# Deformable convolution: a strip sampled in six units instead of two halves, with three weight buffers and the positions on VectorE

## The reference, cut to what matters

```
y0, x0 = floor(yp), floor(xp)            # yp, xp: pixel + tap (ky, kx) + learned offset, 8 groups x 9 taps
val = gather(y0, x0) * (1 - wy) * (1 - wx) + gather(y0, x0 + 1) * (1 - wy) * wx
    + gather(y0 + 1, x0) * wy * (1 - wx) + gather(y0 + 1, x0 + 1) * wy * wx
val = val * mask                         # one mask per pixel, group and tap
out = einsum('bhwkc,kcf->bhwf', val, weight) + bias
out = relu(out) + fine_cal; result = x + out
```

## Time and profile before

| | us |
|---|---|
| median of 3 runs | 3745.19 |
| lowest and highest run | 3737.2 and 3747.83 |
| the profiled execution's own time | 3750.21 |
| its span, first to last instruction | 3748.5 |
| mean granted TensorE clock in it | 0.956 |

### The profile page before, as it was taken

The page is one execution under the profiler, slowest core; times in us unless marked ns, Lnnn a source line. Parts: engine busy times, 40 slices in busy tenths (PEclk is TensorE's granted clock), DMA queues, the critical chain, the costliest instruction groups (busy, mean ns, idle before and its releaser), DMA issues.

```text
span 3748.5 us, 103646 instructions
## 1 busy us (share of the span) xinstructions
PE 3383.5 (90%) x39276; PEld 3082.7 (82%) x39276; DVE 2643.4 (71%) x4029; ACT 1636.7 (44%) x3018; POOL 1300.2 (35%) x1358
## 2 busy tenths in 40 slices
PE   8979999999999947998888998998899898988998
PEld 7869999999999936888787887887788787877888
DVE  3446666666666548878876887886887887688882
ACT  0021211211221215656654665664666665566663
POOL 1000000000000025645645555554654655455451
PEclk9989999999999978999998999998999998999998
DMA  4232232222223221111112111112111112111110
GB/s 160 78 122 42 48 72 42 48 53 39 51 51 43 32 49 30 29 32 31 31 32 32 32 33 29 31 34 32 29 33 31 30 34 36 25 33 32 31 27 23
DMA packets 352248, 159.43 MB, mean 43 GB/s; under 512 B 228724, under 2 KB 346884, under 8 KB 351620
## 3 DMA queue, kind: packets, MB, share of 16 engines
q1 hardware_dynamic: 325456, 109.56, 17.4%
q10 hardware_dynamic: 21724, 26.37, 2.1%
q0 software_dynamic: 4608, 16.78, 1.2%
HBM read 104.60 MB, written 55.23 MB: 43 GB/s over the span
## 4 chain that ended last, share of the span: by engine, by line
PE 44%; issue 7%; ACT 6%; DVE 2%; POOL 2%; ACTq 1%; DMA 1%; SPq 1%; POOLq 0%; DVEq 0%
PE eb L1420 25%; PE tb L981 9%; PE vb L1003 9%; ACT wtT L986 4%; ACT ot L1025 1%; ACT res L1012 1%; DVE wt L975 1%; PE tb L911 1%; DMA win<-cpad 1%; ACTq L1316 1%; PE vb L1018 1%; ACT val L1289 1%; ACTq L882 0%; DVE val L1362 0%; SPq L1083 0%
## 5 line engine op out<-in xcount | busy, mean ns | idle before, releaser
L1420 PE MATMUL eb<-val,wd 128*128 128x256 f32 (+2 forms) x8172 | 1269.5, 300 | 9.5 <-POOL gate L1212 8.5
L1420 PEld LDWEIGHTS eb<-val,wd 128*128 128x128 f32 x8172 | 1080.6, 199 | 44.8 <-issue 35.4
L975 DVE TENSOR_TENSOR wt<-taps_all 128x576 f32<-128x576 f32 x1024 | 938.6, 984 | 52.5 <-PE tb L981 44.6
L981 PE MATMUL tb<-ident,wt 128*128 128x128 f32 x4608 | 715.9, 282 | 63.8 <-ACT wtT L986 45.3
L986 ACT COPY wtT<-tb 128x512 f32<-128x512 f32 x1152 | 651.8, 593 | 164.8 <-PE tb L981 126.0
L1362 DVE TENSOR_TENSOR val<-vb,val 128x432 fp32r<-128x432 f32 (+1 forms) x768 | 382.6, 552 | 411.0 <-ACT val L1289 409.2
L981 PEld LDWEIGHTS tb<-ident,wt 128*128 128x128 f32 x4608 | 504.7, 141 | 185.5 <-ACT wtT L986 103.6
L1289 ACT CAST val<-vb 128x432 fp32r<-128x432 f32 (+1 forms) x768 | 342.1, 524 | 706.4 <-PE vb L1003 706.2
L480 PE MATMUL conv<-fine,wf 128*108 128x256 f32 x4608 | 591.1, 289 | 7.6 <-DVE omT L751 7.6
L480 PEld LDWEIGHTS conv<-fine,wf 128*108 128x108 f32 x4608 | 570.5, 173 | 23.0 <-issue 23.0
L1003 PE MATMUL vb<-wtT,win 64*32 64x144 f32 x16384 | 350.2, 309 | 184.3 <-issue 93.3
(11 more groups left out here) (138 smaller groups left out, 3175.7 us busy)
## 6 DMA issues: line engine op xcount, KB each, us to landing
win<-cpad SPq DMA_DIRECT2D x304, 64.0 KB
om_s<-om_d SPq DMA_DIRECT2D x1152, 12.0 KB
chunk<-in_x SPq DMA_DIRECT2D x32, 512.0 KB, 5.9
xchunk<-in_x SPq DMA_DIRECT2D x32, 512.0 KB, 4.2
r_d<-r POOLq DMA_DIRECT2D x32, 512.0 KB, 3.2
rt<-r_d SPq DMA_DIRECT2D x63, 256.0 KB, 2.9
out<-ot ACTq DMA_DIRECT2D x63, 256.0 KB, 2.2
om_d<-omT SPq DMA_DIRECT2D x64, 216.0 KB
```

The source lines that it names most:

```text
L975: return nc.vector.tensor_tensor(wt[:, g * NK:(g + 1) * NK, WQ * u:WQ * (u + 1)].rearrange("p k (a b) -> p k a b", a=WIN), of_group(0).uns ...
L981: last = nc.tensor.transpose(tb[b][:, 128 * j:128 * j + 128], wt[:, 4 * i + j, :], ident[:])
L1420: done = nc.tensor.matmul(eb[fo][:, W * r0:W * r1], wd[wp][:, half, k, 128 * fo:128 * fo + 128], source[:, at:at + r1 - r0, cols], start=f ...
```

## The change

A strip is cut into six units instead of two halves: unit `at` is tap row d = at // 2 (the three taps of one kernel row, taken in the order 2, 1, 0) of column half hx = at % 2. Each engine's program becomes a loop over slots (strip t, at).

- One unit is 2 product instructions on DVE (768 elements in place of 576), 3 batches of transposes, 64 sampling matmuls of 48 columns (3 taps x 4 rows x 4 pixels) in place of 64 of 144 per half strip, one ACT copy of 768 elements and 2 DVE instructions of 384 elements. So a strip has the same elements but 384 sampling matmuls (768 records) where it had 128 (256 records).
- `wt` and `wtT` are used as three buffers of 12 rows (`n_sub`). In slot (t, at), PE samples the unit of the slot before, and then puts 5, 7 and 6 projection matmuls behind its three batches; DVE makes the products two units ahead.
- `val` has 10 ring rows, so every projection matmul has 256 columns. Two rows are kept twice: SP copies them by 4 DMAs every second strip (`duplicate_rows`), and POOL waits for them (`duplicated`).
- The positions and `coef` go from POOL to DVE (`locate`, slot 5), and the four cap instructions are split over two slots (`begin_cap`, `end_cap`).
- On ACT, `taps` of the next strip's half 0 stands at the end of slot 0 and of half 1 at the end of slot 2. On POOL, `measure` (the distances) stands in slots 0 and 1, behind the edge column `side` of the unit before.
- The window loads are split into a near and a far half (`win_near`, `win_far`); the projection is one strip behind and no longer two, and each output strip has its own PSUM bank `eb[q]`.

Eleven position instructions and two products now stand ahead of the split of unit 5, which opens the next strip's distances on POOL. The core of the diff, in the order sampling helper, PE, DVE, POOL, ACT:

```diff
-        def sample_blocks(v, window):
-
-            for j in range(*THIRDS[v]):
...
+        def sample(sub, b, window):
+
+            for j in range(BLK):
                 for u in range(2):
-                    for g in range(GH):
+                    for c in range(GH):
...
+                        weights = wtT[part, PER * sub:PER * (sub + 1)].rearrange("p (k c) (y x) -> p c k y x", k=3, y=4)
+                        last = nc.tensor.matmul(values_of(b)[32 * c:32 * c + 32, u, :, :, 4 * j:4 * j + 4],
+                                                win[part, window(j), 32 * c:32 * c + 32], weights[:, c, :, :, 4 * j:4 * j + 4],
...
+                def slot(t, p, at):
+                    target, q, pos = unit(t, p, at, -3)
+                    sample_unit(*unit(t, p, at, -1))
+                    for i in range(3):
+                        if known(t, 0, ST):
+                            n = UNITS * t + at
+                            if i == 0:
+                                w(pe, "products", 2 * (n + 1))
+                            w(pe, "tb_out", batch_no(t, at, i) - 1)
+                            transpose_batch(n_sub(at), i, bank_no(t, p, at, i)).then_inc(sems["batched"], 1)
+                        project_part(target, q, pos // 2, pos % 2, i)
...
+                def slot(t, p, at):
+                    products(*unit(t, p, at, 2))
+                    split_values(*unit(t, p, at, -1))
+                    if at in (1, 3):
+                        begin_cap(t + 1, 1 - p, at // 2)
+                    if at in (2, 4):
+                        end_cap(t + 1, 1 - p, at // 2 - 1)
+                    if at == 5:
+                        locate(t + 2, p)
...
+                        for at in range(UNITS):
+                            side(*unit(t, p, at, -1))
+                            if at == 0:
+                                measure(t + 1, 1 - p, 0)
+                            if at == 1:
+                                measure(t + 1, 1 - p, 1)
...
+                    if at == 0:
+                        taps(t + 1, 1 - p, 0)
```

More of the change, by code:

```diff
@@ L1048, in known, with unit @@
                 return not isinstance(v, int) or least <= v < end
+            def unit(t, p, at, ahead):
+                n = at + ahead
+                more, pos = n // UNITS, n % UNITS
+                return t + more, (p + more) % 2, pos
             def loop(e, strips):
@@ L1122, in sp_fast @@
                     load_offsets(sp, s, True, sems["om_loaded"])
-                strip(0, 0, None)
-                for i in range(1, 4):
-                    strip(0, i, i)
-                with sp.Fori(1, 4) as m:
-                    for i in range(4):
-                        strip(0, 4 * m + i, i)
+                batch(0)
                 with sp.Fori(1, B - 1) as b:
@@ L1551, in dve_general @@
                     w(dve, "coef_ready", s + 1)
[L1552 to L1553 removed]
+                    for tile in spare:
+                        nc.vector.memset(tile, 0.0).then_inc(sems["zeroed"], 1)
                     with dve.Fori(0, NWIN) as wy:
```

658 lines of the change are left out of this document (319 added, 339 removed).

## The result

| | before | after |
|---|---|---|
| median of the runs, us | 3744.85 | 4059.45 |
| lowest and highest | 3737.2 and 3747.83 | 4049.04 and 4077.33 |
| span of the profiled execution | 3748.5 | 4058.9 |
| mean granted clock in it | 0.956 | 0.947 |

The change makes the kernel slower by 8.5%: the ratio is 1.0848, with the interval 1.0807 to 1.089. The forecast was 3910, slower by 4.4%. The sign was right and 4059 lies inside the range, but the loss is 315 us where 167 was expected. So a cost was missed that is as large as the whole forecast.

What follows compares the result with a forecast made beforehand. PE was taken to set the end, mostly by its own work. Terms of +2.2 us a strip (+141), +36 for image starts and -10 for the ends gave +167 on 3750, so 3910 us; range 3660 to 4100.

Steps and rivals of the forecast that it cites:

- Sampling: PE's sampling: 768 records of 48 columns at 0.010 us each, in six units of 1.43 us, cost +4.0 us a strip.
- The branch stays: PE's loop over two strips: the gap of 3.11 us at its branch remains, so no term was added.
- The new chain: DVE's split, POOL's edge column and distances, then ACT's taps delay the copy for PE's third batch of slot 1: +2.3 us a strip.
- POOL's addition: In slot 4 POOL's sum follows the edge column and ends after PE wants to turn the result: +0.4 us a strip.
- Pieces: PE's projection: 36 whole matmuls replace 72 pieces of 128 columns every second strip, -1.8 us a strip.
- Bare batches: Five transpose batches with no projection behind them get matmuls and lose 0.77 - 0.42 us each: -1.7 us a strip.
- Ahead of the sampling: PE's 1.65 us wait before sampling goes, six waits of 0.1 for ACT's copy come: net -1.0 us a strip.
- Starts of an image: PE waits for reloaded windows with less work in between: 12 us more at each of three starts, +36 us.
- A: PE's sampling runs at the columns' pace, 0.0052 us a record, so it costs only +0.3 a strip: 3675 us, chance 0.22.
- B: PE's sampling is paced by instruction, 0.0156 us a record, 2.15 us a unit: 4104 us, chance 0.14.
- C: The chain over DVE, POOL and ACT is hidden because DVE is further ahead: 3737 us, no change, chance 0.09.
- D: Waits pull PE's clock down to 1.2 GHz for 3.4 us a strip, costing another 1.7: 4019 us, chance 0.08.

Runs made afterwards that it cites:

- the kernel before with thirds: The kernel before with each sampling matmul of 144 columns cut into three of 48, all else unchanged; 4425.5 us, ratio 1.184.

## Why the prediction was right in sign and short by half

The forecast of 3910 was 149 us too low. That 4059 still lies in the range is luck in part: a cost of some 250 us was missing from the sum, the other terms together were some 100 us too dear, and the range's upper end was drawn for the chain, the duplicated rows and the clock.

*Sampling, forecast +4.0 a strip:* measured +3.24 in records; a unit is 1.30 to 1.31 us and not 1.43. The step from the burst of eight to a rate for 128 in a row was sound: 0.010 was a little over what a unit shows. The Trainium skill (TensorE: Matmul & The Clock Gate, Part 3) would have tiles side by side cost one matmul plus about 4 ns for each further one. The trace does not bear that out for a stream in which a weight load goes with each: 9.5 ns a record at 48 columns.

*What failed is the step "The branch stays" and all that it stands for.* The prediction had seen 3.11 us in which nothing released PE, and took it for a fixed price of the branch. It was the visible part of a supply with a limit of its own. The page of before has the queue of instructions in it, 361 packets; the change multiplies PE's instructions by 1.8, and no term of the sum was for that. It costs +3.34 us a strip inside the sampling and +0.59 inside the projection, together some 250 us. The forecast came out only 150 us short because other terms were too dear, above all the chain and the sampling's records.

*The new chain, forecast +2.3:* it is there, in the slot and with the releasers that were named. ACT waits for POOL's distance:

```profile
2513.40 1.17 ACT L960 ACTIVATE taps_all<-taps_all 128x1152 f32<-128x1152 f32 x1 [3.30 <-POOL taps_all L955]
```

and PE stops ahead of the third batch of slot 1 at 2517.09. But PE's wait for ACT's copies is 75.6 us in all, 1.2 a strip. One reason is that slot 1 of the odd strips has a late page of its own (1.19 us at 2514.27), which shifts what PE wants to later; with half the sampling instructions the same wait is 125.0 us, 2.0 a strip. But it is there in 31 of the 32 odd strips and in only 14 of the even ones, and why it is missing there stays open. (The prediction's own terms add up to 11.3 to 12.3 for ACT's copy, not 11.4 to 12.4.) The distances on POOL took 1.85 and 1.89, at the dear end of the estimate.

*POOL's addition, forecast +0.4 (0 to +0.9):* measured +0.75. *Pieces, forecast -1.8:* -1.48 between the two kernels, -2.1 in the run that undoes them. *Bare batches, forecast -1.7:* the stops of 1.39 us a strip that ACT's copies caused are gone, but late pages put 0.69 back. *Ahead of the sampling, forecast -1.0:* -1.32 with the image starts in it, which are 0.35 of the other sign, so -1.7 without them.

*Starts of an image, forecast +36:* the wait for the windows goes from 17.2 to 39.6 us, **+22**. Of that, 3.4 stand at the very first sampling; the three starts make 36.2, **+19**. They are 10 to 13 us each and not 18:

```profile
2079.50 1.79 PE L1012 MATMUL vb<-wtT,win 64*32 64x48 f32 x128 [10.51 <-DMA win<-cpad]
```

*Ends, forecast -10:* the first sampling starts 1.2 us later, and from the last one to the end of the span are 40.1 us instead of 47.4: -6. *Hidden edits, forecast 0:* the positions take 3.1 us on DVE, from 2503.45 to 2506.59, in place of the 3.2 assumed; in no list of PE's waits do DVE's positions or the duplicated rows appear among the large entries.

*The rivals.* A and B fall by the distance of records. C (the chain is hidden) falls, since PE waits for it, though its removal alone gains only 10 us, within noise. D (the clock is pulled down) is real, but small between these two kernels: the granted clock is 0.947 for the whole execution against 0.956, and 0.94 against 0.96 in the stretch of the earlier trace rows. Behind the stop of 3.07 us at 2540.04 the clock is at 1.2 GHz for 3.4 us, and seven projection matmuls take 1.84 us where they took 1.10 in the slots before:

```profile
2542.01 1.84 PE L1461 MATMUL eb<-val,wd 128*128 128x256 f32 x7
```

The stage has 287 us at that level against 195 before. By the records at both levels I estimate 77 us lost against 63, so 14 us of the 315, where D wanted 1.7 a strip, 109 us. The same sum gives some 90 us in the kernel before with thirds and 37 us of what writing out before's loop gained.

## What to carry to other kernels

Count the instructions an engine takes per microsecond, not only their busy time: if a change multiplies an engine's instructions, read the instruction queue's packets on the page and look for stops without a releaser, which stand at the same matmul in every turn of a loop. What counts is how fast a page is used up: here one of 256 instructions that PE got through in under 3 us ended in a stop nearly every time. A wait that goes may have been covering such a stop, so an order that removes it alone may gain nothing; try it together with what thins the instructions out. And try the cheap thing first: writing out PE's loop was worth 2.2% here.

## What the runs showed of the hardware that was not expected

- PE's instructions come in pages of 256. In the changed kernel with its loop written out, 110 of 111 stops over 0.5 us inside one kind of work (242.9 us) stand at a multiple of 256 instructions, most of them 1 to 3 us long.
- A page's packet starts 1.2 us (median) behind PE's first matmul of the page before, takes 1.0 us, and PE uses the page 1.4 us after it landed if it had to wait for it. Of 93 pages that PE used up in under 3.0 us, 88 were followed by a stop.
- A branch back over two strips costs PE about 3 us: 28 issue waits, 93.3 us, gone when the loop is written out, with 80 us of the time. By estimate 37 us of what is gained come by the clock, which is 0.971 in place of 0.956.
- At a granted clock of 0.50, a transpose starts 213 ns after the last, at 1.00 it is 109 ns (medians). The mean distance of sampling records of 48 columns is 12.8 ns at the lower level and 9.4 at the higher (after), of 144 columns 28.2 and 15.0 (before).
- A sampling matmul with its weight load costs 9.5 ns a record at 48 columns, 12.6 at 96 and 15.8 at 144 in the changed kernel and its two variants: three times the columns are 1.7 times the time.
- A projection matmul of 128 columns starts 112 ns after the last, one of 256 columns 122 ns (medians).
- Cutting a stream of 128 records on 64 x 32 tiles into two of 64, with full-array work between them, costs 0.48 us a unit.
